# Second pass of a perceiver layer: two of the small unit's six key pairs scored by one matmul each

## The reference, cut to what matters

```python
qh = (q @ Wq.T + bq).reshape(B, Sq, N_HEAD, D_HEAD)      # Sq = 128, N_HEAD = D_HEAD = 16
kh = (k @ Wk.T + bk).reshape(B, Sk, N_HEAD, D_HEAD)      # Sk = 12544
vh = (v @ Wv.T + bv).reshape(B, Sk, N_HEAD, D_HEAD)
scores = jnp.einsum('bqhd,bkhd->bhqk', qh, kh) / np.sqrt(D_HEAD)
scores = jnp.where(attention_mask[:, None, :, :], NEG_FILL, scores)
probs = jax.nn.softmax(scores, axis=-1)
out = jnp.einsum('bhqk,bkhd->bqhd', probs, vh)
```

## Time and profile before

| | |
|---|---|
| median of three runs | 475.36 us |
| profiled execution | 475.08 us |
| its span, first to last instruction | 473.4 us |
| mean granted TensorE clock | 0.993 of full speed |
| TensorE matmul busy | 448.7 us, 95% of the span |
| ScalarE busy | 384.1 us, 81% |
| VectorE busy | 347.9 us, 73% |

### The profile page before, as it was taken

How to read it: one execution, slowest core, us unless ns; L and a number is a source line. 1 busy time by engine, 2 the same in 40 slices (tenths; PEclk the granted TensorE clock), 3 DMA queues, 4 the chain that set the end, 5 groups by cost and what they waited for, 6 DMA issues and landing times.

```text
span 473.4 us, 16042 instructions
## 1 busy us (share of the span) xinstructions
PE 448.7 (95%) x6464; PEld 353.3 (75%) x6464; DVE 347.9 (73%) x483; ACT 384.1 (81%) x436; POOL 100.2 (21%) x101
## 2 busy tenths in 40 slices
PE   7899999999999999996999999999999999999896
PEld 4776667766677676772698999999999999985463
DVE  5779999999999999999479988445555434605566
ACT  6688888888888888875698999999999999992433
POOL 1599533333333334306000000000000000000000
PEclk9999999999999999997999999999999999999999
DMA  7997656765557755948988698778789878100000
GB/s 252 345 384 264 223 207 246 296 247 214 213 212 295 285 216 209 363 188 287 422 316 289 242 329 295 272 264 297 259 287 331 279 276 268 70 3 1 1 2 15
DMA packets 33259, 112.01 MB, mean 237 GB/s; under 512 B 4048, under 2 KB 10576, under 8 KB 33232
## 3 DMA queue, kind: packets, MB, share of 16 engines
q1 hardware_dynamic: 29056, 105.07, 60.0%
q0 software_dynamic: 4032, 6.42, 4.7%
q10 hardware_dynamic: 144, 0.13, 0.1%
HBM read 74.44 MB, written 33.96 MB: 229 GB/s over the span
## 4 chain that ended last, share of the span: by engine, by line
PE 69%; DVE 11%; ACT 8%; issue 7%; SPq 2%; DMA 1%; POOL 0%; ACTq 0%; DVEq 0%; POOLq 0%
PE ps_a L1112 21%; PE ps_k L1126 20%; PE ps_a L967 10%; PE ps_k L958 10%; PE ps_a L1001 4%; ACT early L513 3%; DVE block_max L716 3%; DVE early L721 3%; ACT k_stack L466 1%; DMA ctx_b<-in_ctx 1%; DVE early L752 1%; ACT k_hi L497 1%; PE ps_a L1292 1%; PE ps_k L1309 1%; PE ps_a L1012 1%
## 5 line engine op out<-in xcount | busy, mean ns | idle before, releaser
L716 DVE TENSOR_REDUCE block_max<-ps_a 128x2 f32<-128x896 f32 x112 | 120.9, 1083 | 0.0
L1112 PEld LDWEIGHTS ps_a<-q_stack,k_stack 64*128 64x128 f32 x1568 | 96.3, 187 | 14.2 <-issue 12.5
L1112 PE MATMUL ps_a<-q_stack,k_stack 64*128 64x128 f32 x1568 | 105.5, 279 | 0.8 <-DVE q_stack L762 0.4
L513 ACT CAST early<-ps_a 128x896 bf16<-128x896 f32 x104 | 94.7, 910 | 6.1 <-PE ps_a L1001 6.1
L584 ACT ACTIVATE middle<-ps_a 128x1536 f32<-128x1536 f32 (+1 forms) x56 | 90.2, 1663 | 10.1 <-PE ps_a L1112 10.1
L584 ACT ACTIVATE early<-ps_a 128x1536 f32<-128x1536 f32 (+1 forms) x56 | 90.2, 1663 | 5.0 <-PE ps_a L1112 5.0
L967 PE MATMUL ps_a<-w_hi,k_stack 128*128 128x256 f32 x392 | 68.5, 297 | 0.0
L721 DVE TENSOR_TENSOR early<-early 128x896 bf16<-128x896 bf16 x104 | 65.6, 631 | 0.6
L958 PE MATMUL ps_k<-k_stack,w_hi 128*128 128x448 f32 x224 | 60.7, 391 | 2.7 <-issue 1.3
L967 PEld LDWEIGHTS ps_a<-w_hi,k_stack 128*128 128x128 f32 x392 | 53.0, 188 | 11.3 <-issue 11.2
L1001 PE MATMUL ps_a<-k_hi,q_pair 32*128 32x448 bf16 x448 | 42.7, 370 | 10.9 <-ACT early L513 8.7
(11 more groups left out here) (198 smaller groups left out, 495.9 us busy)
## 6 DMA issues: line engine op xcount, KB each, us to landing
k_stack<-k_hi_scratch SPq DMA_DIRECT2D x68, 448.0 KB, 5.2
v_scratch<-early SPq DMA_DIRECT2D x14, 952.0 KB, 5.2
v_in<-v_scratch SPq DMA_DIRECT2D x14, 952.0 KB, 5.3
k_hi_scratch<-k_hi SPq DMA_DIRECT2D x28, 448.0 KB, 2.5
k_lo_scratch<-k_lo SPq DMA_DIRECT2D x16, 448.0 KB, 3.2
k_stack<-k_lo_scratch SPq DMA_DIRECT2D x16, 448.0 KB, 5.2
ctx_b<-in_ctx SPq DMA_DIRECT2D x7, 896.0 KB, 6.8
early<-in_ctx SPq DMA_DIRECT2D x6, 896.0 KB, 7.0
```

What stands on the lines that cost most here:

```text
L513: nc.scalar.copy(staged[:, u % 2], pair_scores(u, 0)).then_inc(max_copied, 1)
L716: nc.vector.tensor_reduce(block_max[:, 2 * u:2 * u + 2, par], pair_scores(u, 1), AX.X, ALU.max).then_inc(max_taken, 1)
L1112: last = nc.tensor.matmul(ps_a[:, base + bank, at * Q:(at + 1) * Q], k_stack[half, b_par, a, t * P:(t + 1) * P], q_stack[half, a, ab, :], ...
```

## The change

`WIDE = 2`: in the small unit, pairs 0 and 1 are now scored by one matmul each, on all 128 partitions, with the pair's 256 query columns (both heads') moving; since `q_stack` is zero in the other head's rows, columns 0 to 127 come out as the scores of head 2a and columns 128 to 255 as those of head 2a+1. They fill bank 1. Pairs 2 to 5 write bank 0 with their first half and bank 2 with their second, so no bank is shared, and the semaphore `shared_scored`, its increment and its wait are gone. The small unit has 2 + 8 matmuls in place of 12. The large unit, `add_up`, the loops and all other engines' programs are the same.

```diff
+WIDE = 2
...
-        shared_scored = sem("shared_scored")
...
         def cell(u, k, ab):
             if UP[u % 2] == 8:
                 return 2 * ab + k // 4, k % 4
-            if ab == 0:
-                return (1, k) if k < 2 else (0, k - 2)
-            return (2, k) if k < 4 else (1, k - 2)
+            return (1, 2 * k + ab) if k < WIDE else (2 * ab, k - WIDE)
...
-                def score(b_par, u, shared):
+                def score(b_par, u):
...
-                    for k, (t, a) in enumerate(GROUPS[u]):
+                    wide = WIDE if UP[u % 2] == 6 else 0
+                    for k, (t, a) in enumerate(GROUPS[u][:wide]):
+                        nc.tensor.matmul(ps_a[:, base + 1, 2 * k * Q:(2 * k + 2) * Q], k_stack[:, b_par, a, t * P:(t + 1) * P],
+                                         q_stack[:, a, :, :], start=not masked, stop=True, skip_group_check=True)
+                    for k, (t, a) in enumerate(GROUPS[u][wide:], wide):
                         for ab in range(2):
                             bank, at = cell(u, k, ab)
-                            if UP[u % 2] == 6 and (k, ab) == (4, 1):
-                                pe.wait_ge(shared_scored, shared)
                             half = slice(ab * PAIR_ROWS, (ab + 1) * PAIR_ROWS)
                             last = nc.tensor.matmul(ps_a[:, base + bank, at * Q:(at + 1) * Q],
                                                     k_stack[half, b_par, a, t * P:(t + 1) * P], q_stack[half, a, ab, :],
                                                     start=not masked, stop=True, skip_group_check=True)
-                            if UP[u % 2] == 6 and (k, ab) == (1, 0):
-                                last.then_inc(shared_scored, 1)
                     last.then_inc(scored, 1)
```

More of the change, by code:

```diff
@@ L1156, in two_blocks @@
                                     arrive(i * 2 + 1, 1, 1)
-                                score(nxt // UNITS, nxt % UNITS, i * UNITS + w // 2 + 2)
+                                score(nxt // UNITS, nxt % UNITS)
                         if u % UNITS == 0:
@@ L1168, in attend @@
                     pe.wait_ge(second_rows_set, u + 1)
-                    score(0, u, 1)
+                    score(0, u)
                 for _ in range(WARM_PASS):
```

## The result

| | before | after |
|---|---|---|
| median of the runs, us | 475.09 (4 runs) | 480.48 (4 runs) |
| profiled execution, us | 475.08 | 480.39 |
| its span, us | 473.4 | 478.7 |
| ratio of after to before | | 1.0107, 95% interval 1.0074 to 1.0140 |

The changed kernel is slower by 1.1%. The forecast was 481.2 us, its own range 479.8 to 482.4.

The account below looks back on a forecast made before the run. TensorE was taken as the bound, held by ScalarE in every other step. Per step 0.06 + 0.10 + 0.05 added, 0.05 + 0.055 removed: +5.7 us over 54 steps, +0.2 us at the start; forecast 481.2 us, own range 479.8 to 482.4.

Parts of the forecast that it names:

- The wide form gains nothing by itself: Small unit's scores: a steady 128-row matmul takes 0.12 us, against 0.112 for a pair of half-array matmuls.
- The wide entry, +0.06: Start of a step's scores: first to second wide matmul takes 0.22 us where a pair has 0.16.
- rival C: One term less: wide entry at 0.16 or re-entry hidden, +2.8 to +3.1 us, about 478.3 us; chance 0.09.
- The change of form, +0.10: Inside the small unit, from 128-row to 64-row matmuls: 0.21 us against the pair's 0.112.
- rival A: Changing the row count is free: +0.5 us, 475.9 us, no change that can be told; chance 0.05.
- The second entry, +0.05: First 64-row pair after the wide matmuls: weights exposed, 0.16 us to the next pair in place of 0.112.
- The wait, -0.05: Small unit's pair 5: the wait on `shared_scored` goes, 0.05 us less a step.
- ScalarE's hold, -0.055, with 0.10 to spare: Large unit's start: ScalarE's exponentials no longer hold TensorE in every other step, -0.055 us on average, 0.10 to spare.
- The sum: Scores 1.92 against 1.81 us a step, +5.7 us over 54 steps; profiled execution 481.0 us.
- the pause at 256 us: Second pass's loop: one pause at 256.96 us, counted as 0.86 us of the loop's time before the change.
- B: Faster: row-count change free and wide entry at a pair's 0.16, -1.1 us, 474.3 us; chance 0.05.

Follow-up runs that it names:

- experiment 3: Changed kernel with all six pairs of the small unit scored by wide matmuls, the large unit as it was; median 483.07 us, ratio to before 1.0146.
- experiment 8: Kernel with all pairs of both units wide, plus the large unit's exponential split in two; median 476.56 us, ratio to before 1.0033.
- experiment 4: Changed kernel with the two wide matmuls last in the small unit instead of first; median 488.38 us, ratio to before 1.0268.
- experiment 2: Changed kernel with every pair of both units scored by one 128 x 256 matmul; median 481.44 us, ratio to before 1.0117.
- experiment 1: Kernel before without the shared-bank wait, second halves of pairs 4 and 5 overwriting other areas, no wide matmuls; median 474.94 us, ratio 1.0003.
- experiment 5: Kernel before with the large unit's exponential split into two instructions, each with its own semaphore, wait kept; median 473.13 us, ratio 0.9948.
- experiment 6: Changed kernel with the large unit's exponential split in two; median 480.17 us, ratio to before 1.0091.
- experiment 7: Kernel before with the split exponential and the large unit's pair 0 scored between the small unit's pairs 3 and 4; median 470.46 us, ratio 0.9891.

## Why the prediction was right

*The wide form gains nothing by itself.* Right: 0.008 us more than a pair for each (experiments 3 and 8), as L967 had it. That shape stood in another stage of the same kernel, and its rate carried over.

*The wide entry, +0.06.* Right: 308.31 - 308.09 = 0.22 us, and rival C is out. The weight loads themselves do not differ: the first of a run lasts 186 ns for 128 rows and 183 for 64, and the second starts 0.11 us after it in both forms (308.08 to 308.19, 308.51 to 308.62). What differs is the first matmul behind them, up to 390 ns against 274 for the next wide one, and 323 against 272 with 64 rows: 0.11 to 0.12 and 0.05 us more. So the entries differ though the loads do not. Why 128 rows keep the first matmul back for longer, no run shows.

*The change of form, +0.10.* Right within 0.01: 0.20 us from the last wide matmul to the first 64-row pair, against 0.21 from the row of 32. This term and the next had no row of their own, only a nearest one. Experiment 4 shows it by itself and in the other direction too, and rival A is out. What the trace shows of it: the first 64-row load starts 0.20 us after the last wide matmul, where in experiment 2 a wide load in a row of its kind starts together with the matmul before it (both at 310.55), and the load engine idles 0.13 us a step (7.2 us in 54). The runs price the change; what happens inside it is not shown.

*The second entry, +0.05.* Right: 0.163 us from the first 64-row pair to the next. That its weights are exposed the trace shows: their loads start together with their matmuls at 308.51, after the load engine's 0.13 us without work. That nothing is in flight ahead of them holds for loads alone: the last wide matmul is recorded to 308.31 + 0.27 = 308.58, an end that is modelled.

*The wait, -0.05.* Right: 1.71 against 1.76 in the short steps of experiment 1.

*ScalarE's hold, -0.055, with 0.10 to spare.* Right that it goes: it is a cost of the kernel before (experiment 5) that the kernel after doesn't have (experiment 6). The 0.10 was too much, for it was counted up to the matmul. The exponential ended 0.07 us before the weight load was due (0.08 as the median of the steps), and before the change TensorE went on 0.04 after an exponential, so 0.03 to 0.04 us were to spare. That the hold was gone all the same is a narrow hit. The same arithmetic failed in experiment 2, where the load runs 0.12 us ahead of its matmul.

*The sum.* 1.916 against 1.92 us for the scores, 5.6 against 5.7 us for 54 steps. The profiled execution came 0.6 us under the sum (480.4 against 481.0): 0.1 from the steps, 0.8 from the pause at 256 us, which shrank, less 0.3 for a later first score and a longer tail. The last three are outside the mechanism and none was forecast, so that the total came so close owes something to luck. I had let the pause stand as it was. Whether it shrinks because the steps are longer was not tried. In experiment 1, where they are shorter, it is down to 0.36, so I leave its cause open.

*What the rivals were worth.* B, the faster one, needed both a free change and a cheap entry. Neither holds. A's 475.9 us was worked out only for the case without the re-entry; with it, at 1.83 us a step and no hold, it would have been +0.02 x 54, about 476.4 us. It is out either way.

## What to carry to other kernels

In this kernel a matmul that uses the whole array is no faster than two halves that run side by side (0.12 against 0.112 us), and mixing the two forms in one run of matmuls costs 0.09 to 0.10 us at each change, with 0.05 (64 rows) or 0.10 (128 rows) more behind it. The small wait (0.05 us) was cheaper here than the change of form that avoids it (0.10); moving one independent piece of work in front of the waiting instruction removed it without any other cost to TensorE (experiment 7 against 5). What a matmul waited for was wanted here by its weight load, 0.06 us (64 rows) to 0.12 us (128 rows) ahead of the matmul in a steady run: in experiment 2 the exponential ended at 310.77 and the load went at 310.82. And where steps come in two lengths by turns, another engine may be holding this one, as ScalarE was here (1.76 and 1.87 us before, 1.75 in both steps of experiment 5): look for it before counting what a removed wait brings.

## What I had not expected

That splitting ScalarE's instruction for the large unit, which gives the engine more to do (ACT busy 384.1 us before, 387.4 in experiment 7), would be worth 0.058 us a step (1.812 to 1.754), three times what removing the wait alone brings (0.019): only the time at which its first half is ready matters to TensorE. Once the hold is gone, the moved pair is worth nearly as much (1.754 to 1.708). And pauses of up to 1.6 us on TensorE that no semaphore explains occur in the loop's first round, at other places in each kernel: 0.97 us in the kernel before, 0.16 in the one after, 0.36 in experiment 1, 1.1 and 0.96 in experiment 5, 0.4 in experiment 6, 0.4, 0.2 and 1.6 in experiment 7, none in experiments 2 to 4 and 8. Experiment 6 has one of 0.3 in the last round too. Their cause is open. They limit what a comparison of single traces can tell to about 1 us, unless the steps are compared without them.
